# Gate and up products as three rounded products, value projections among the first maxima of attention, fewer and larger transfers of keys and rows of maxima

## The chip, the cores and the metric

The kernel runs on one core of a Trainium2 chip. Its time is the device time of one execution in microseconds, the median of several runs; lower is better. One further execution is profiled, and its trace is what the rows below come from.

## The reference, cut to what matters

A residual stream `x` of 2048 tokens by 256 features passes eight layers. What the change touches:

```python
# first layer (A): attention, 16 heads of 16; masked scores become zero and stay in the softmax
scores = einsum('bthd,bshd->bhts', q, k) * tril
out = einsum('bhts,bshd->bthd', softmax(scores / T ** 0.5), v).reshape(B, T, 256) @ Wo
# feed-forward, run twice (after A, and after the linear layer)
gate = einsum('bsd,hd->bsh', x, w_gate)          # hidden 1024
up = einsum('bsd,hd->bsh', x, w_up)
y = einsum('bsh,dh->bsd', silu(gate) * up, w_down)
# linear layer ("lin"): k * v summed over the tokens so far, times q, then a projection
# differential attention (B): every token sees every other; two score products with a factor lambda
# attention with latent keys and rotary parts (C): causal
# hyperbolic layers ("hyp", "hypout"): one projection, scaled by a tanh of its norm
```

Every layer is added to `x`, and its input is `x` normalised per token. All is float32.

## The kernel before

**Stages.** The program is written out in order: `start` (normalisation "in" and the projections "p0" of A), attention A, a wave of "o0", "ffn", "lin", "ffn", then the projections "p1" of B, attention B, a wave of "o1", "hyp", "p2", attention C, and "o2" with "hypout". Outside attention the tokens go in four chunks of 512 (`NC` = 4, `CH` = 512). In a wave, each layer follows the one before by two chunks, so that TensorE has another layer's chunk while a normalisation runs on VectorE. A chunk's normalised input is transposed on TensorE (`norm_transposes`, after the main work of the next step) and copied by ScalarE to `HT` (`norm_copies`).

**Feed-forward.** For each of eight blocks `m` of 128 hidden features, TensorE makes a gate bank and an up bank of PSUM, each from two float32 products of 128x512 (`over_k`, line 740). A float32 product stands in the trace as two records. ScalarE takes a tanh of the gate (L1035), VectorE makes the gated product in two instructions (L1196, L1200), and line 842 multiplies by the down weights. Four banks go round.

**Projections p0, p1.** TensorE makes four banks of queries and keys (`PARTS_ORDER`) and two of values (`token_major` into `VV`, four float32 products of 128x256 in each bank). VectorE splits every bank of queries and keys into a rounded part and a rest (L1169, L1170) in one of two buffers `STG`, and SyncE's queue (SP) stores both in DRAM; VectorE may fill a buffer only when its store has landed. From there SP loads queries (`load_q`, 6 transfers for a cell) and keys (`load_k`, 12 transfers of 64 KB for each half of the heads and each chunk). A matmul on tiles of type float32r reads numbers already rounded, and makes one record.

**Attention.** A cell is a chunk of 512 queries and a group of four heads; 16 cells follow each other. `Layer.plan` writes one list, `steps`, which all engines walk: "max" (TensorE makes two banks of scores, line 885, and VectorE takes their maxima, L1289 or L1292; two slots of two banks), "neg" (GpSimd negates and splits the 16 maxima of a token, `NM`), "mtr" (TensorE transposes them, line 895, ScalarE copies them to `MR`), after which SP writes them as two more rows of the queries (`max_rows`, 4 transfers a cell, line 502), "score" (line 924: scores minus their maximum, then exp by ScalarE, L1054), "pv" (line 953: times the values), and "otr", "rec", "suf" at the end of a cell. TensorE keeps the order of the list: the first "score" of a cell waits for that cell's rows of maxima, and what stands behind it waits too. The rows of ones that go with the keys are written by `one_rows`, once for each half.

**SP before the first score of a layer** goes through: keys of the last chunk (first half), ones of the second half, a wait for everything ScalarE has taken, queries of the fourth slot (into a part of `HT`), keys of the second half (one chunk of them for A and C, all four for B), then the rows of maxima of cell 0. Weights for the hyperbolic layers are loaded right after attention A, 15 transfers (lines 563 to 571).

Of the kernel before, what the change touches and what calls it, by code (L numbers as in the profile page):

```python
# [23 lines left out]
F32 = mybir.dt.float32  # L24
# [7 lines left out]
P = 128  # L32
# [7 lines left out]
HG = 4  # L40
# [40 lines left out]
class Layer:  # L81
# [59 lines left out]
    def plan(self):  # L141
# [46 lines left out]
        self.steps += due[0][at:]  # L188
        self.ring, self.at, self.n_taken = {}, {}, 0
# [8 lines left out]
def build(nc, a, out):  # L198
# [3 lines left out]
    with ctx:  # L202
# [29 lines left out]
        NEG = sb("NEG", [P, HG, BPC])  # L232
        OT4 = OS[:, 0:BPC * HG * VW].rearrange("p (b j d) -> p b j d", b=BPC, j=HG)
# [5 lines left out]
        NM = sb("NM", [P, HG, PARTS, BPC])  # L239
# [11 lines left out]


# [86 lines left out]
        mask_low = sem("mask_low")  # L339
# [14 lines left out]
        HAS_NORM = {"in", "o0", "ffn", "lin", "o1", "hyp", "o2"}  # L354

# [7 lines left out]
        BANKS = {"in": (0, 0), "wt": (0, N_TRANSPOSED), "p0": (4, 2), "p1": (4, 2), "p2": (8, 3), "o0": (2, 2), "o1": (2, 2), "o2": (2, 2),  # L363
                 "ffn": (18, 0), "lin": (6, 2), "hyp": (2, 0), "hypout": (2, 0)}
        D_COUNT, A_COUNT, HT_AT = {}, {}, []
        NORM_OF = {}
        d_total, a_total = 0, 0
        for kind, steps in PROGRAM:
            if steps is None:
                D_COUNT[kind], A_COUNT[kind] = d_total, a_total  # L370
                continue
# [20 lines left out]
        K_DMAS = 16 * 12  # L392
        Q_DMAS = 16 * 6
        ROW_DMAS = 16 * HG
# [12 lines left out]
        def _(sp):  # L407
# [86 lines left out]
            def max_rows(L, n):  # L494
# [3 lines left out]
                k = PARTS * BPC  # L498
# [19 lines left out]

            def attention(L):
# [34 lines left out]
            for kind, steps in PROGRAM:  # L554
                if steps is None:
                    attention(att[kind])
                    if kind == "A":

                        sp.wait_ge(L0.out_done, len(L0.cells))
                        for dst, src in ((W2["q"], km(a["L1b_q"])), (W2["o"], km(a["L1b_o"])), (WN, km(a["hyp_w"])),  # L560
                                         (SCALE, a["hyp_scale"].partition_broadcast(P)),
                                         (WKV, km(a["kv"])), (WKUP, a["kup"]), (WVUP, a["vup"])):
                            sp.dma_start(dst, src).then_inc(w2_in, 16)
                        half = ROPE // 2
                        for i in range(2):
                            for h in range(2):
                                o = half * (h if i == 0 else 1 - h)
                                dst = slice(o, o + half)
                                src = slice(half * h, half * (h + 1))
                                sp.dma_start(WQR[i][:, :, dst], km(a["qr"])[:, :, src]).then_inc(w2_in, 16)  # L570
# [812 lines left out]
```

## Time and profile before

| | us |
|---|---|
| median of 3 runs | 2762.98 |
| lowest and highest of them | 2744.1, 2763.98 |
| profiled execution, its time | 2726.22 |
| its span, first to last instruction | 2724.5 |
| TensorE busy | 2514.2 (92%) |
| VectorE busy | 1836.6 (67%) |
| ScalarE busy | 1332.6 (49%) |
| GpSimd busy | 239.1 (9%) |
| mean granted TensorE clock | 0.931 |

The profiled execution took 36.8 us less than the median. Sums made on the trace stand against 2726.22 us; what they give is then taken off the median.

### The profile page before, as it was taken

Reading aid. Unit: us, or ns where it says so; the run is one execution under the profiler, and the core shown is the slowest. Engines: PE = TensorE matmul, PEld = TensorE weight load, DVE = VectorE, ACT = ScalarE, POOL = GpSimd, SP = SyncE. Lnnn points to the kernel's source line nnn. Section 1 sums busy time; section 2 is a strip of 40 time slices with the busy share of each in tenths; the row PEclk is TensorE's granted clock in tenths of the full one; section 3 lists DMA queues with packets and bytes.
Section 4 is the critical chain, followed back from the end, with each engine's and each line's share of the span. In section 5 each row is a group of like instructions: output and inputs, shape, how many; then the busy total and the mean of one; then the engine's idle time right before and its main releaser. Section 6 shows DMA issues by size and latency. Waiting matters only on the chain.

```text
span 2724.5 us, 46506 instructions
## 1 busy us (share of the span) xinstructions
PE 2514.2 (92%) x17992; PEld 1253.4 (46%) x17992; DVE 1836.6 (67%) x4042; ACT 1332.6 (49%) x2678; POOL 239.1 (9%) x767
## 2 busy tenths in 40 slices
PE   7699999989999998899999999976879999999995
PEld 5354444445655564244444444343345544444444
DVE  5557788815355535899999999658657676666508
ACT  2246677861111110388888888840035444455551
POOL 0332212110000000000000000000022111010100
PEclk9568799999999998599999999997789999999998
DMA  8410000000000006300000000002721000000000
GB/s 248 107 32 18 13 13 8 2 20 1 1 0 1 16 0 187 55 13 7 14 13 8 13 8 7 2 16 77 214 66 31 13 15 8 7 2 7 5 29 32
DMA packets 61407, 90.55 MB, mean 33 GB/s; under 512 B 13441, under 2 KB 25985, under 8 KB 61057
## 3 DMA queue, kind: packets, MB, share of 16 engines
q1 hardware_dynamic: 61184, 87.57, 11.6%
q8 instruction: 142, 2.33, 0.3%
q14 instruction: 81, 0.66, 0.1%
HBM read 54.76 MB, written 31.46 MB: 32 GB/s over the span
## 4 chain that ended last, share of the span: by engine, by line
PE 74%; DVE 13%; SPq 4%; ACT 3%; DMA 3%; issue 2%; POOL 0%; DVEq 0%; POOLq 0%; ACTq 0%
PE PS L953 19%; PE PS L885 14%; PE PS L740 13%; PE PS L924 11%; PE PS L935 7%; PE PS L842 4%; DVE MP L1292 3%; ACT PF L1054 3%; PE PS L933 2%; SPq L476 2%; DVE WC L1289 1%; DVE JUNK L1289 1%; DVE ST L1126 1%; SPq L487 1%; DVE KF L1133 1%
## 5 line engine op out<-in xcount | busy, mean ns | idle before, releaser
L1054 ACT ACTIVATE PF<-PS 128x512 f32<-128x512 f32 (+3 forms) x2304 | 1169.3, 560 | 618.2 <-PE PS L935 341.1
L1292 DVE TENSOR_REDUCE MP<-PS 128x2 f32<-128x1024 f32 x704 | 849.5, 1222 | 80.2 <-PE PS L885 74.6
L953 PE MATMUL PS<-PF,VX 128*32 128x256 f32 (+3 forms) x9216 | 708.4, 385 | 0.1
L885 PE MATMUL PS<-KFR,QRR 48*128 48x512 f32 (+3 forms) x1920 | 487.5, 512 | 55.5 <-DVE MP L1289 17.1
L924 PE MATMUL PS<-QRR,KFR 50*128 50x512 f32 (+3 forms) x1920 | 405.3, 418 | 30.6 <-DMA QRR<-MR 14.0
L885 PEld LDWEIGHTS PS<-KFR,QRR 48*128 48x128 f32 x1920 | 191.2, 199 | 406.7 <-issue 240.9
L953 PEld LDWEIGHTS PS<-PF,VX 128*32 128x32 f32 x9216 | 190.5, 110 | 337.0 <-issue 238.4
L924 PEld LDWEIGHTS PS<-QRR,KFR 50*128 50x128 f32 x1920 | 187.8, 192 | 113.3 <-ACT PF L1054 90.1
L740 PE MATMUL PS<-HT,WA 128*128 128x512 f32 x512 | 221.1, 592 | 0.0
L935 PE MATMUL PS<-WAR 128*128 128x512 f32 (+3 forms) x640 | 215.5, 418 | 0.0
L1289 DVE CUSTOM_DVE_ANT_0 JUNK<-PS,WB 128x512 bf16<-128x512 f32 (+2 forms) x224 | 131.3, 586 | 114.9 <-PE PS L885 99.5
L670 POOL TENSOR_SCALAR_AFFINE_SELECT PF<-PF 128x128 f32<-128x128 f32 x512 | 142.5, 292 | 549.0 <-ACT PF L1054 544.4
L740 PEld LDWEIGHTS PS<-HT,WA 128*128 128x128 f32 x512 | 96.6, 190 | 118.6 <-issue 115.7
L935 PEld LDWEIGHTS PS<-WAR 128*128 128x128 f32 x640 | 95.8, 189 | 97.3 <-issue 90.7
L997 ACT COPY HT<-PS 128x512 f32<-128x512 f32 x64 | 34.6, 588 | 213.9 <-PE PS L774 213.9
L1289 DVE CUSTOM_DVE_ANT_0 WC<-PS,WB 128x512 bf16<-128x512 f32 (+2 forms) x224 | 130.1, 581 | 0.0
L1141 DVE TENSOR_TENSOR X<-PS,X 128x512 f32<-128x512 f32 x48 | 33.1, 690 | 135.4 <-PE PS L842 99.5
L1035 ACT ACTIVATE PF<-PS 128x512 f32<-128x512 f32 x64 | 38.2, 597 | 167.5 <-PE PS L740 167.5
L933 PE MATMUL PS<-WAR 64*128 64x512 f32 (+3 forms) x320 | 116.7, 365 | 0.0
L933 PE MATMUL PS<-WCR,WAR 64*128 64x512 f32 (+3 forms) x320 | 116.6, 364 | 0.0
L842 PE MATMUL PS<-WA,KF 128*128 128x256 f32 x512 | 111.8, 379 | 0.0
L1289 DVE CUSTOM_DVE_ANT_0 JUNK<-PS,X 128x512 bf16<-128x512 f32 (+1 forms) x96 | 64.2, 669 | 63.3 <-PE PS L885 60.1
(139 smaller groups left out, 2223.2 us busy)
## 6 DMA issues: line engine op xcount, KB each, us to landing
KFR<-parts_a_k SPq DMA_DIRECT2D x96, 64.0 KB, 3.1
KFR<-parts_b_k SPq DMA_DIRECT2D x96, 64.0 KB, 3.6
KFR<-parts_c_k SPq DMA_DIRECT2D x96, 64.0 KB, 3.1
QRR<-parts_a_q SPq DMA_DIRECT2D x78, 64.0 KB, 2.3
QRR<-parts_b_q SPq DMA_DIRECT2D x78, 64.0 KB, 2.3
QRR<-parts_c_q SPq DMA_DIRECT2D x78, 64.0 KB, 2.3
parts_a_q<-PF SPq DMA_DIRECT2D x8, 512.0 KB, 3.8
parts_a_k<-PF SPq DMA_DIRECT2D x8, 512.0 KB, 3.7
```

Of the source, the lines that this page charges most:

```text
L476: sp.dma_start(x.rearrange("d (r t) -> d r t", r=PAIRS)[:, :, t], head_rows(L, "k", PRODUCTS[product][1], h, g, t))\
L670: g_.affine_select(out=tile, in_=tile, compare_op=ALU.is_ge, fill=0.0, base=0, pattern=[[1, P]], channel_multiplier=-1).then_inc(L.mask_do ...
L740: ins = mm(dst, left(k), right(k), start=k == 0, stop=k == n - 1)
L842: ins = mm(bank(b, D, i * D), GT[:, m, blk(2 * h + i)], WDT[:, m, :], start=m == 0, stop=m == HID // P - 1)
L885: ins = mm(bank(slot + h, w), Q[rows, t0:t0 + P], KS[rows, o:o + w], start=True, stop=True)
L924: ins = mm(bank(4 + (e + h) % RING2, CH - off), KS[rows, o:o + P], Q[rows, t0 + off:t0 + CH], start=True, stop=not L.rope)
L933: mm(bank(4 + (e + h) % RING2, CH - off), RS[half, ROPE_K[1], sb_ * P:(sb_ + 1) * P], q, start=False, stop=False)
L935: mm(bank(4 + (e + h) % RING2, CH - off), RS[:, ROPE_K[0], sb_ * P:(sb_ + 1) * P], RS[:, ROPE_Q[0], c * CH + off:(c + 1) * CH], start=Fals ...
L953: ins = mm(PS[32 * j:32 * j + 2 * DH, 7 * CH + t0:7 * CH + t0 + size], VX[:, v0:v0 + 2 * DH], PT[:, u % SETS, j, t0:t0 + size], start=firs ...
L1054: sc.activation(PT[:, u % SETS, j, off:CH], bank(4 + e % RING2, CH - off), ACT.Exp).then_inc(L.taken, 1)
L1289: ins = v.tensor_tensor_reduce(out=junk[h][:, 0:w], in0=src[:, h], in1=other, scale=1.0, scalar=low, op0=ALU.mult if L.zeros else ALU.add, ...
L1292: ins = v.reduce_max(dst, src, AX.X)
```

## The change

**Gate and up.** Each float32 product becomes three float32r products of the same 128x512 shape: rounded weights with rounded input, rounded weights with the input's rest, the weights' rest with rounded input. The rounded weights `WGU[0]` are made by ScalarE, one 128x512 copy in each of the first eight units of A's last cell. The rests `WGU[1]` are made by GpSimd, eight 128x512 subtractions after its last step of A. For the chunks that feed a feed-forward layer (normalisations after "o0" and "lin"), `norm_copies` takes each transposed bank twice, once rounded and once whole (into unused room in the values' tile), and GpSimd subtracts (two 128x512 for a chunk). TensorE waits for `wgu_ready` once and for `ht_rest` before each feed-forward chunk.

**Values.** p0 and p1 no longer make the values. They are eight steps ("value", c, h) spread over the steps before the first "mtr" of A and B: one bank each, four float32 products of 128x256, and a copy by ScalarE. SP loads the fourth slot of queries only after they are all taken, and so does TensorE start its first "mtr".

**Transfers.** `load_k` issues 6 transfers of 128 KB for a half and a chunk instead of 12 of 64 KB; `max_rows` issues 2 instead of 4 (`NM` is laid out by halves for it).

**Order on SP.** Keys of the second half now come before the fourth slot of queries. For B the ones of the first half are written again, since the rounded weights lay there, and the 15 transfers of hyperbolic weights move from the end of A to between B's fourth slot of queries and B's first rows of maxima.

```diff
+        if not self.rope:
+            products = [("value", c, h) for c in range(NC) for h in range(BPC // 2)]
+            room = self.steps.index(("mtr", 0)) - 1
+            for i, step in reversed(list(enumerate(products))):
+                self.steps.insert(1 + i * room // len(products), step)
...
+        WGU = [KS[:, i * 4096:(i + 1) * 4096] for i in range(2)]
+        HTL = [QS[:, i * KD * CH:(i + 1) * KD * CH].rearrange("p (k t) -> p k t", k=KD) for i in range(3)]
+        HTL.append(WCR[:, 0:KD * CH].rearrange("p (k t) -> p k t", k=KD))
...
-                    for g in (2 * half, 2 * half + 1):
-                        x = KS[row:row + DH, g * PAIRS * T:(g + 1) * PAIRS * T].bitcast(F32)
-                        sp.dma_start(x.rearrange("d (r t) -> d r t", r=PAIRS)[:, :, t], head_rows(L, "k", PRODUCTS[product][1], h, g, t))\
-                            .then_inc(L.k_in[half][c], 16)
+                    x = KS[row:row + DH, half * 2 * PAIRS * T:(half + 1) * 2 * PAIRS * T].bitcast(F32).rearrange("d (x t) -> d x t", t=T)
+                    src = scr[L.name, "k"][PRODUCTS[product][1], half * 2 * HG * DH:(half + 1) * 2 * HG * DH, t]
+                    sp.dma_start(x[:, :, t], src.rearrange("(x h d) t -> h d x t", h=2, d=DH)[h]).then_inc(L.k_in[half][c], 16)
...
-                for j in range(HG):
-                    row = HALF * (j % 2) + MROW
-                    dst = Q_AT[L.q_slot[n][0]][row:row + PARTS, j // 2 * CH:(j // 2 + 1) * CH].bitcast(F32)
-                    sp.dma_start(dst.rearrange("i (n t) -> i n t", t=P), MR[j * k:(j + 1) * k, :]).then_inc(L.max_rows_in, 16)
+                for h in range(2):
+                    row = HALF * h + MROW
+                    dst = Q_AT[L.q_slot[n][0]][row:row + PARTS].bitcast(F32)
+                    sp.dma_start(dst.rearrange("i (x t) -> i x t", t=P), MR[h * k:(h + 1) * k, :]).then_inc(L.max_rows_in, 16)
...
                 one_rows(1, ones_in[1 + "abc".index(L.name)])
-                sp.wait_ge(a_free, A_COUNT[L_KEY[L.name]])
-                load_q(L, QRING - 1)
+                if L is L1:
+                    one_rows(0, ones_back)
+                sp.wait_ge(a_free, A_BEFORE[L_KEY[L.name]])
                 load_k(L, 1, 0)
                 if not L.causal:
                     for c in range(1, NC):
                         load_k(L, 1, c)
+                sp.wait_ge(a_free, A_COUNT[L_KEY[L.name]])
+                load_q(L, QRING - 1)
+                if L is L1:
+                    hyperbolic_weights()
...
+                        for i in range(8):
+                            w = slice(i * CH, (i + 1) * CH)
+                            pool.wait_ge(wgu_high, i + 1)
+                            g_.tensor_tensor(WGU[1][:, w], WA[:, w], WGU[0][:, w].bitcast(F32), ALU.subtract).then_inc(wgu_ready, 1)
...
+                        for kk in range(KD):
+                            by_head = lambda x: x.rearrange("p (b h d) -> p b h d", h=H, d=DH)
+                            g_.tensor_tensor(by_head(low[:, kk, :]), whole(pending[1], pending[0], kk),
+                                             by_head(HTR[:, pending[0], kk, :].bitcast(F32)), ALU.subtract).then_inc(ht_rest, 1)
...
                     for m in range(HID // P):
-                        for W in (WGT, WUT):
+                        for w in range(2):
                             b = d_bank()
-                            over_k(bank(b), lambda kk: W[:, kk, m * P:(m + 1) * P], ht).then_inc(d_ready, 1)
+                            for kk in range(KD):
+                                o = w * 2048 + kk * HID + m * P
+                                high, rest = WGU[0][:, o:o + P], WGU[1][:, o:o + P]
+                                mm(bank(b), high, HTR[:, c, kk, :], start=kk == 0, stop=False)
+                                mm(bank(b), high, low[:, kk, :], start=False, stop=False)
+                                ins = mm(bank(b), rest, HTR[:, c, kk, :], start=False, stop=kk == KD - 1)
+                            ins.then_inc(d_ready, 1)
...
+                    if step[0] == "value":
+                        _, c, h = step
+                        W, b = (W0 if L is L0 else W1A)["v"], a_bank()
+                        for i in range(2):
+                            t0 = (2 * h + i) * P
+                            ins = over_k(bank(b, D, i * D), lambda kk: HT[:, c, kk, t0:t0 + P], lambda kk: W[:, kk, :])
+                        ins.then_inc(a_ready, 1)
...
+                    if kind in SPLIT:
+                        take(HTR[:, c, k, :], bank)
+                        na.k -= 1
+                        take(whole(kind, c, k), lambda b: bank(b).rearrange("p (b h d) -> p b h d", h=H, d=DH)).then_inc(a_free, 1)
...
+                        if L.zeros and n == len(L.cells) - 1 and r == 1 and u - L.first[n] < 8:
+                            w = slice((u - L.first[n]) * CH, (u - L.first[n] + 1) * CH)
+                            sc.copy(WGU[0][:, w], WA[:, w]).then_inc(wgu_high, 1)
```

## Rows read from the trace of the kernel before

**Rows 1.** Stretches by stage: length, busy of each engine, granted clock, DMA share, GB/s

```profile
75.00:103.00 28.00, 10.38 (x35) 4.84 (x35) 15.44 (x71) 0.60 (x3) 11.97 (x18) 0.51 0.61 133
617.00:1025.00 408.00, 402.57 (x1315) 239.29 (x1314) 192.30 (x493) 57.85 (x100) 1.94 (x8) 1.00 0.01 3
...
1079.00:1124.00 45.00, 30.52 (x79) 11.33 (x81) 43.68 (x40) 0.25 (x1) 0.67 (x3) 0.50 0.73 127
```

**Rows 2.** Chain of waits, first feed-forward chunk, gate and up: start, length, line, records

```profile
617.62 27.47 PE PS L740 x64
```

**Rows 3.** Timeline of TensorE in C: four rounded products in a row, and two

```profile
2139.13 1.19 PE L745 MATMUL PS<-WAR 128*128 128x512 f32 x4
...
2421.45 0.73 PE L935 MATMUL PS<-WAR 128*128 128x512 f32 x2
2422.11 0.64 PE L953 MATMUL PS<-PF,VX 128*32 128x256 f32 x8
```

**Rows 4.** Timeline of p1: VectorE's wait for a store, SP's load of queries

```profile
1041.20 8.24 SPq L487 DMA_DIRECT2D QRR<-parts_b_q  x18
...
1052.79 0.69 DVE L1169 TENSOR_SCALAR PF<-PS 128x512 fp32r<-128x512 f32 x1 [9.94 <-DMA parts_b_q<-PF]
```

**Rows 5.** Timeline of A's start: transposed maxima, SP's queue, first score

```profile
86.68 5.90 SPq L487 DMA_DIRECT2D HTR<-parts_a_q  x6
...
87.86 0.25 ACT L1063 COPY MR<-PS 32x128 f32<-32x128 f32 x1 [11.12 <-PE PS L895]
...
98.31 2.57 SPq L502 DMA_DIRECT2D QRR<-MR  x4
...
102.03 0.80 PE L924 MATMUL PS<-QRR,KFR 50*128 50x512 f32 x2 [10.70 <-DMA QRR<-MR]
```

**Rows 6.** Timeline of p1 and of B's start: values, maxima, SP's queue, first score

```profile
1043.47 3.62 PE L740 MATMUL PS<-WB,HT 128*128 128x256 f32 x16
...
1096.00 22.86 SPq L476 DMA_DIRECT2D KFR<-parts_b_k  x48
...
1107.37 9.13 DVE L1292 TENSOR_REDUCE MP<-PS 128x2 f32<-128x1024 f32 x8
...
1118.99 2.62 SPq L502 DMA_DIRECT2D QRR<-MR  x4
...
1123.62 0.79 PE L924 MATMUL PS<-QRR,KFR 50*128 50x512 f32 x2 [1.42 <-DMA QRR<-MR]
```

**Rows 7.** Timeline after A: first and last of 15 transfers; copies of the first input

```profile
595.68 0.39 SPq L563 DMA_DIRECT2D WC<-in_L1b_q  x1
...
604.11 0.49 SPq L571 DMA_DIRECT2D WC<-in_kr  x1
...
610.24 1.07 ACT L997 COPY HT<-PS 128x512 f32<-128x512 f32 x2 [5.65 <-PE PS L774]
```

**Rows 8.** Timeline of C's start: transposed maxima, keys on SP, the wait

```profile
1965.46 5.44 SPq L476 DMA_DIRECT2D KFR<-parts_c_k  x12
...
1975.54 0.25 ACT L1063 COPY MR<-PS 32x128 f32<-32x128 f32 x1 [15.66 <-PE PS L895]
...
1983.55 5.55 SPq L476 DMA_DIRECT2D KFR<-parts_c_k  x12
...
1991.61 0.48 PE L885 MATMUL PS<-KFR,QRR 48*128 48x128 f32 x2 [12.01 <-DMA KFR<-parts_c_k]
```

**Rows 9.** Groups of instructions: busy, mean ns, idle before; a copy, a GpSimd addition

```profile
L997 ACT COPY VX<-PS 128x512 f32<-128x512 f32 x24 | 14.1, 586 | 152.9 <-PE PS L740 152.9
L635 POOL TENSOR_TENSOR WC<-WC,VX 128x272 f32<-128x272 f32 x24 | 18.2, 760 | 1.6
```

**Rows 10.** Stretches of attention A, columns as in the first group

```profile
560.00:572.00 12.00, 10.96 (x108) 3.43 (x100) 0.00 (x0) 10.27 (x20) 0.20 (x1) 1.00 0.01 1
...
133.00:188.00 55.00, 53.43 (x340) 30.89 (x344) 29.44 (x77) 22.30 (x57) 16.60 (x48) 0.50 0.14 37
215.00:256.00 41.00, 38.45 (x390) 18.77 (x390) 34.58 (x81) 27.01 (x63) 12.21 (x41) 1.00 0.07 21
```

More of the change, by code:

```diff
@@ L238, in build @@
         MX = sb("MX", [P, 2, HG, BPC])
[L239 removed]
+        NM = sb("NM", [P, 2, PARTS, PAIRS, BPC])
         EM = sb("EM", [P, 2, HG, BPC])
@@ L250, in build, with whole @@
         bank = lambda b, n=CH, o=0: PS[:, b * CH + o:b * CH + o + n]
+        WGU = [KS[:, i * 4096:(i + 1) * 4096] for i in range(2)]
+        HTL = [QS[:, i * KD * CH:(i + 1) * KD * CH].rearrange("p (k t) -> p k t", k=KD) for i in range(3)]
+        HTL.append(WCR[:, 0:KD * CH].rearrange("p (k t) -> p k t", k=KD))
+        def whole(kind, c, k):
+            b = 2 * (KD * (SPLIT[kind] + c % 2) + k)
+            return VV[:, b:b + 2, :, 0:DH]
         GT = QF[:, 0:4096].rearrange("p (m t) -> p m t", t=CH)
@@ L369, in build @@
             if steps is None:
-                D_COUNT[kind], A_COUNT[kind] = d_total, a_total
+                D_COUNT[kind], A_BEFORE[kind] = d_total, a_total
+                if not att[kind].rope:
+                    a_total += NC * BPC // 2
+                A_COUNT[kind] = a_total
                 continue
@@ L517, in load_rope_q, with hyperbolic_weights @@
                 sp.dma_start(RQ2[ROPE:P, c % 2, :].bitcast(F32), scr_r["q"][0][:, t]).then_inc(L.rope_q_in[c % 2], 16)
+            def hyperbolic_weights():
+                sp.wait_ge(L0.out_done, len(L0.cells))
+                for dst, src in ((W2["q"], km(a["L1b_q"])), (W2["o"], km(a["L1b_o"])), (WN, km(a["hyp_w"])),
+                                 (SCALE, a["hyp_scale"].partition_broadcast(P)),
+                                 (WKV, km(a["kv"])), (WKUP, a["kup"]), (WVUP, a["vup"])):
+                    sp.dma_start(dst, src).then_inc(w2_in, 16)
+                half = ROPE // 2
+                for i in range(2):
+                    for h in range(2):
+                        o = half * (h if i == 0 else 1 - h)
+                        dst = slice(o, o + half)
+                        src = slice(half * h, half * (h + 1))
+                        sp.dma_start(WQR[i][:, :, dst], km(a["qr"])[:, :, src]).then_inc(w2_in, 16)
+                        sp.dma_start(WKR[i][:, dst], a["kr"][:, src]).then_inc(w2_in, 16)
             def attention(L):
@@ L556, in _ @@
                     attention(att[kind])
[L557 to L570, printed above, removed]
-                                sp.dma_start(WKR[i][:, dst], a["kr"][:, src]).then_inc(w2_in, 16)
                     continue
@@ L979, in _ @@
                     if pending is not None:
-                        norm_of[c] = pending
+                        norm_of[c] = pending, k
+                    if k in SPLIT:
+                        rest_of[c] = rests.next()
                 assert pending is None
@@ L998, in take, with take_values @@
                 return sc.mul(dst, src, scale)
+            def take_values(c, h):
+                b0 = BPC * c + 2 * h
+                take(VV[:, b0:b0 + 2, :, 0:DH], lambda b: bank(b).rearrange("p (b h d) -> p b h d", h=H, d=DH)).then_inc(a_free, 1)
             def weight_copies():
@@ L1023, in main @@
                     take(CKV[:, c % 2, :], lambda b: bank(b)[0:LATENT]).then_inc(a_free, 1)
-                if k in ("p0", "p1", "p2"):
+                if k == "p2":
                     for h in range(2):
-                        b0 = BPC * c + 2 * h
-                        take(VV[:, b0:b0 + 2, :, 0:DH], lambda b: bank(b).rearrange("p (b h d) -> p b h d", h=H, d=DH)).then_inc(a_free, 1)
+                        take_values(c, h)
                 if k == "ffn":
@@ L1038, in main, with norm_copies @@
                     sc.activation(NW[:, 5, :], NW[:, 4, :], ACT.Tanh).then_inc(n2_tanh, 1)
-            def norm_copies(c):
+            def norm_copies(c, kind):
                 for k in range(KD):
-                    take(HT[:, c, k, :], bank).then_inc(a_free, 1)
+                    if kind in SPLIT:
+                        take(HTR[:, c, k, :], bank)
+                        na.k -= 1
+                        take(whole(kind, c, k), lambda b: bank(b).rearrange("p (b h d) -> p b h d", h=H, d=DH)).then_inc(a_free, 1)
+                    else:
+                        take(HT[:, c, k, :], bank).then_inc(a_free, 1)
             def attention(L):
@@ L1057, in attention @@
                             sc.activation(EM[:, n % 2], MX[:, n % 2], ACT.Exp, scale=-1.0).then_inc(L.weight_done, 1)
+                    if step[0] == "value":
+                        take_values(*step[1:])
                     if step[0] == "mtr":
@@ L1088, in _ @@
                     if pending is not None:
-                        norm_copies(pending)
-                    pending = c if k in HAS_NORM else None
+                        norm_copies(*pending)
+                    pending = (c, k) if k in HAS_NORM else None
         @block.vector
```

44 lines of the change are left out of this document (29 added, 15 removed).

## The prediction

> **What bounds the kernel now.** I read the stretches by stage first [rows 1]. In the first feed-forward wave TensorE is busy 402.6 of 408 us at full granted clock: what it saves there is saved. At the starts of attention A and B it is busy 10.4 of 28 and 30.5 of 45 us at half clock: something else sets the pace. The chain of waits shows gate and up of a feed-forward chunk as one unbroken piece [rows 2]. The timelines then say what ends last elsewhere. In p1 VectorE waits 9.94 us for a store that SP could issue only behind 18 loads of queries [rows 4]. In A the transposed maxima lie in `MR` at 88.1, but SP still issues queries and then keys and comes to them at 98.31; TensorE idles 10.70 us and scores at 102.03 [rows 5]. In B VectorE's maxima set the pace, and SP is through its 48 loads of keys at 1118.9, just in time for the rows of maxima at 1118.99 [rows 6]. In C the maxima are ready at 1975.8, and TensorE waits for keys to 1991.6 [rows 8].
>
> **Gate and up.** Now 64 records take 27.47 us, 0.429 each: two passes of 512 columns [rows 2]. After, it is 96 records a chunk of one pass each. Price of one: four rounded 128x512 products on 128 rows last 1.19 us together and two last 0.73, so each further one costs (1.19 - 0.73)/2 = 0.23 us [rows 3]. 96 x 0.23 = 22.1 us, 5.4 less; eight chunks (four in each of two runs) give **-43 us**. The lower end, half a float32 record (0.215), gives 20.6 us and -55; the upper end is rival 1. I take 0.23, the row of the same shape.
> The Trainium skill ("TensorE: Matmul & The Clock Gate", Back-to-back issue gap) gives column count over 2.4 GHz plus about 2.5 ns, 216 ns; by it the term would be -54. The trace's four in a row disagree with it by 14 ns each, and the trace decides.
> VectorE and ScalarE don't become the bound: they are busy 192 and 58 of the wave's 408 us [rows 1]. Down and the normalisations stay.
>
> **Making the halves.** In A's last cell ScalarE makes 20 exps, five units of four, in 12 us, and is busy 10.27: 2.05 of each unit of 2.4 [rows 10]. Eight units get a copy of 0.586 more [rows 9]. Between nothing left over (all fits the idle 0.35 but 0.24, so 2) and 8 x 0.586 = 4.7, I take **+4**: the exps feed three banks in a ring, so the idle time is in slivers. Nothing at all is its lowest end.
> GpSimd's eight subtractions: 272 columns take 0.760 [rows 9], so 512 some 1.43, together 11.5 us from A's end near 596 [rows 7], to 608. The first chunk's transposed input is copied by 611.3 now [rows 7], by 612.5 with two copies more; two subtractions end near 615.5, before TensorE's first gate product at 617.6 [rows 2]: hidden by 2 us. The same two copies delay the "o0" chunk behind them once. Together **+1.5**, ends 0 and 5. Later chunks have a whole step of cover, 14 us or more. If that cover were gone at the first chunk, it would cost what rival 4 says.
> No row shows GpSimd beside a VectorE instruction with two SBUF inputs. The Trainium skill ("SBUF — State Buffer", SBUF: two separate sides) says that such a pair takes turns for a whole instruction; the short steps of the normalisation before 617 are of this kind. By it two to four turns of 1.43 would be added, 3 to 6 us once.
>
> **Values.** Removed from p0 and p1: 3.62 us of TensorE a chunk, some 1.7 a bank [rows 6]. It lies beside VectorE's wait for stores [rows 4], so taking it away gives nothing there. Added: eight banks before the first "mtr".
> *A.* Eight values and nine maxima. TensorE has idled before, so the clock starts at half (0.51 in this stretch [rows 1]). Two values at half clock are 6.8, six at full 10.3, the maxima and what lies between some 3.5: from 74.4 the last value is copied at about 95.5. Before, TensorE sat idle until 102, so most of this is free. SP has waited: queries 2.9, two rows 1.3, landing 1.1 (102.03 less the end of SP's 2.57, 100.88 [rows 5]), first score near 101 against 102.03: **-1**. Ends: all values at full clock, 96 (-6); all at half, 112 (+10).
> *B.* Here VectorE paces: a maximum each 1.14 us (9.13/8 [rows 6]). TensorE works one maximum ahead, which covers about 1.2 us of a value; a value costs VectorE 1.7 - 1.2 = 0.5 at full clock and 3.4 - 1.2 = 2.2 at half. At the mean, 1.35 x 8 = 10.8 us. Thirty maxima stand before or between the values: 1079.4 + 34 + 10.8 = 1124 for the last one. Behind its copy (0.6) SP issues, in order: six transfers of queries (22.86/48 = 0.48 each, 2.9), the 15 of hyperbolic weights (595.68 to 604.60, 8.9 [rows 7]), two rows of maxima 1.3, and the landing 2 (1123.62 less 1121.61 [rows 6]). That is 1124 + 15.7 - 1 (p1, below) = 1139, against 1123.6: **+15**, ends +8 and +22. Behind the waiting score stand all further maxima, so VectorE stops too; nothing makes this up.
>
> **Transfers.** A transfer of 64 KB costs SP 0.48 us, one of 4 KB 0.64 (2.57/4 [rows 5]): its size doesn't show, so I take 0.48 for 128 KB; the bound is 0.96, no saving. In p0 and p1 most waits end with a landing of the same bytes: -1 each, in the two sums above. In C, between 1965.46 and the rows of maxima, 24 loads of keys become 12 and 4 rows 2: 12 x 0.47 + 2 x 0.64 = 6.9, all on the path, since the maxima are ready at 1975.8 [rows 8]. Within p2 SP's queue is in the way now and then: -2. C: **-9**, ends 0 and -12. Other late rows of maxima, half as many transfers each: **-2**.
>
> **Sum.** -43 + 4 + 1.5 - 1 + 15 - 9 - 2 = -34.5 us; the profiled execution would be 2726.2 - 34.5 = 2692, the median 2763 - 34 = **2729 us**. About 1% (27 us) is what a measurement of this kernel can tell from no change: its runs lie 20 us apart, the profiled one 37 below the median. One likely reason stands in the trace: A has long stretches at either clock, and does 390 matmuls in 41 us at full, 340 in 55 at half [rows 10]. By that 55 us at half are worth about 19.
>
> **Rivals.**
> 1. *The weights don't hide (slower than before).* The stage breaks even when a rounded product costs 27.47/96 = 0.286 us, the whole sum at 0.274. Two rounded products take 0.66 from their start to the next matmul, 0.33 each [rows 3]; if all 96 paid that, a chunk would take 31.7 us, +4.2 x 8 = +34 in place of -43, and the median would be 2806. Against it: the further ones of a row cost 0.23 in the same rows, so the 0.33 holds one exposed weight load and not two.
> 2. *The waits of B and A eat the gain.* Half clock throughout the first maxima: A +10, B +22, the rest as above: -16 us, 2747. For it: both stretches stand near 0.50 now, though TensorE was busy two thirds of B's. Against: the values are dense work.
> 3. *The starts cost little, a rounded product 0.22.* A -6, B +8, gate and up -50: -53 us, 2710. Earlier full clock in A would add to it.
> 4. *GpSimd is late.* At twice its row, 31 us for ten subtractions in place of 14.4, +14 at the wave's start: 2743.
>
> **How the numbers follow.** Forecast as summed 0.48; rival 3 and beyond (clocks in A, down to 2680) 0.20; rivals 2 and 4 together 0.24; rival 1 0.08. Of the forecast's own spread (2713 to 2745) two thirds lie below 2735, the 1% line, and of rivals 2 and 4 a sixth: faster 0.32 + 0.20 + 0.04 = 0.56. Slower by over 1% (above 2790): rival 1 and a hundredth of bad clocks, 0.09. The same: 0.35. The range leaves out rival 1 and the far ends: 2682 to 2765.
>
> **What the profile after would show.** Chain of waits: gate and up near 22.1 us a chunk, 96 records; 31.7 would be rival 1. From the first maximum to the first score some 26 us in A, as now, and 60 us in B in place of 44, with the hyperbolic transfers right before the rows of maxima on SP. C's keys of the second half some 7 us sooner. A first gate product at most 5 us later behind A's end; a wait on GpSimd there would be rival 4. What would make me wrong: another price of a rounded product in a dense stream, a clock that doesn't rise under the values, a 128 KB transfer that costs SP twice as much, or long stretches of A at another clock than now.

## The result and the profile after

The changed kernel takes 2788.64 us (median of 12 runs) against 2763.22 us for the kernel before on the same chip (12 runs): 1.0116 times as long, interval 1.0082 to 1.0149. It is slower by 1.2%, where 2729 us was forecast. Every ratio compares fast executions alone, those within 1.5% of a kernel's fastest (one of 5169 us, whose cause isn't known, is left out here), and the profiled executions of e1 and e2 were slower ones with mean clocks of 0.907 and 0.900, so that of these two no attention's time is used.

The profiled execution took 2766.02 us (span 2764.3), 39.8 us above that of before. To see where, I took the start of the first instruction of each stage from the timelines of both kernels:

| stage | before | after | change | forecast |
|---|---|---|---|---|
| start to A's first score | 102.03 | 103.05 | +1.0 | -1 |
| A, first score to end | 493.85 | 495.67 | +1.8 | +4 |
| A's end to first gate product | 21.6 | 25.2 | +3.6 | +1.5 |
| first gate product to end of last down | 407.2 | 391.95 | -15.3 | -43 |
| last down to B's first maximum | 54.7 | 78.8 | +24.2 | -1 |
| B's first maximum to first score | 44.2 | 68.1 | +23.9 | +16 |
| B, first score to end | 672.9 | 666.5 | -6.4 | (-2, all rows of maxima) |
| B's end to C's first score | 196.5 | 199.1 | +2.6 | -9 |
| C and what is behind it | 731.5 | 735.8 | +4.4 | 0 |

The two stages before B's first score cost 48.1 us together, three times what the feed-forward wave gives back. Outside the three attentions the profiled executions of all kernels agree within some 4 us in a stage where nothing was edited, so this table tells more than the whole time does; the +2.6 before C's first score is within that spread by itself.

The stretches by stage, as [rows 1] of before (us, busy of TensorE, weight loads, VectorE, ScalarE, GpSimd, granted clock, DMA share, GB/s):

```profile
624.00:1016.00 392.00, 368.57 (x1565) 288.36 (x1564) 205.12 (x492) 64.22 (x114) 18.25 (x22) 0.99 0.01 3
1016.00:1095.00 79.00, 33.25 (x81) 14.20 (x79) 28.62 (x57) 2.15 (x4) 0.00 (x0) 0.74 0.68 176
1095.00:1163.00 68.00, 47.13 (x143) 26.48 (x145) 44.19 (x39) 4.97 (x9) 0.67 (x3) 0.68 0.36 58
```

In the wave TensorE now has 23 us without work, where it had 5 [rows 1]. Its groups of instructions there (busy, mean ns, idle before and what ended it) name the place, and VectorE's groups name a second thing:

```profile
L879 PE MATMUL PS<-HTR,KFR 128*128 128x512 f32 x256 | 104.7, 409 | 13.3 <-DVE PF L1268 13.3
```
```profile
L1186 DVE TENSOR_SCALAR NW<-NW 128x4 int32<-128x4 int32 x13 | 8.8, 678 | 0.4
L1200 DVE TENSOR_SCALAR NW<-MV 128x4 f32<-128x4 f32 x13 | 8.7, 668 | 0.4
```

The timeline of one such stall, on GpSimd, VectorE and TensorE:

```profile
625.94 2.37 POOL L742 TENSOR_TENSOR QRR<-VX,HTR 128x512 fp32r<-128x512 f32 x2 [6.31 <-ACT VX L1055]
```
```profile
626.27 0.90 DVE L1200 TENSOR_SCALAR NW<-MV 128x4 f32<-128x4 f32 x1
627.20 1.13 DVE L1186 TENSOR_SCALAR NW<-NW 128x4 int32<-128x4 int32 x1
628.36 0.17 DVE L1187 TENSOR_SCALAR NW<-NW 128x4 int32<-128x4 int32 x1
...
630.34 1.38 DVE L1205 TENSOR_SCALAR KF<-X,MV,NW 128x256 f32<-128x256 f32 x4
631.64 0.68 DVE L1268 SCALAR_TENSOR_TENSOR PF<-PF,PS 128x512 f32<-128x512 f32 x1
```
```profile
632.37 0.50 PE L879 MATMUL PS<-HTR,KFR 128*128 128x512 f32 x1 [2.59 <-DVE PF L1268]
```

TensorE is one step ahead: it fills the four banks of gate and up while VectorE still normalises another chunk, and then waits until VectorE comes to the first of them (L1268). While GpSimd's two subtractions run, two VectorE instructions on four columns take 0.90 and 1.13 us; the third, behind them, takes 0.17. Only 7 of the 13 normalisations in the wave meet a subtraction; the others take what they took before.

The stalls cost more than their own length. There are six of 2.5 to 2.8 us in the wave, and at the end of three of them (from 719.9, 818.9 and 849.6 us) the granted clock falls to the lower of its two levels, 1.2 GHz, for a few us. The first of these, right behind a wait of 2.55 us for L1268 (columns as above):

```profile
720.00:724.00 4.00, 4.00 (x12) 3.09 (x12) 1.94 (x4) 0.60 (x1) 0.00 (x0) 0.58 0.01 4
```

Gate products start 0.43 us apart there and 0.235 before and behind. The three stretches last 10.2 us together and so cost about 5 us, an estimate from these two rates. In the kernel before and in e5 below the clock stays at 2.4 GHz through the wave.

At B's start the timeline of SP and of TensorE (as [rows 6]) and the chain of waits between them say what ends last:

```profile
1070.88 5.92 SPq L496 DMA_DIRECT2D KFR<-parts_b_k  x8
1076.84 8.26 SPq L456 DMA_DIRECT2D KFR<-ONE  x4
1085.15 13.38 SPq L496 DMA_DIRECT2D KFR<-parts_b_k  x24
1148.61 2.63 SPq L506 DMA_DIRECT2D HTR<-parts_b_q  x6
...
1160.09 1.41 SPq L521 DMA_DIRECT2D QRR<-MR  x2
```
```profile
1094.75 0.79 PE L932 MATMUL PS<-KFR,QRR 48*128 48x512 f32 x2 [33.89 <-DMA KFR<-ONE]
1095.47 3.62 PE L778 MATMUL PS<-WB,HT 128*128 128x256 f32 x8
...
1138.57 1.99 PE L778 MATMUL PS<-WB,HT 128*128 128x256 f32 x8
...
1162.83 0.80 PE L980 MATMUL PS<-QRR,KFR 50*128 50x512 f32 x2 [5.68 <-DMA QRR<-MR]
```
```profile
1078.22 4.29 SPq L456
1082.55 11.85 DMA KFR<-ONE
1094.75 0.79 PE PS L932 x2
```

B's first maximum waits for the ones that are written again; they are issued behind all keys of the first half, and the last lands 11.85 us after its issue. Then come the values: seven of eight banks take 2.9 to 3.8 us, one 1.99. In the gap between 1151.25 and 1160.09 stand the 15 hyperbolic weights. C's start, as [rows 8]:

```profile
2007.76 6.95 SPq L496 DMA_DIRECT2D KFR<-parts_c_k  x6
...
2017.65 1.30 SPq L521 DMA_DIRECT2D QRR<-MR  x2
```
```profile
2026.49 0.47 PE L932 MATMUL PS<-KFR,QRR 48*128 48x128 f32 x2 [13.99 <-DMA KFR<-parts_c_k]
2028.44 0.80 PE L980 MATMUL PS<-QRR,KFR 50*128 50x512 f32 x2 [1.47 <-DMA QRR<-MR]
```

SP's six transfers of second-half keys took 6.95 us in place of 5.55 for twelve, and TensorE still waits for keys long after SP has issued them. The first score then waits for the rows of maxima, which SP has issued by 2018.9.

### The profile page after: what moved, and what is told of

Same layout as the page of the kernel before. It is cut to its first block, busy times and chain, and to the rows that moved or that the text cites. A ratio compares the mean times of both kernels' runs of the same rounds, so it can differ in the third digit from the quotient of the medians.

```text
span 2764.3 us, 46832 instructions
## 1 busy us (share of the span) xinstructions
PE 2481.3 (90%) x18248; PEld 1306.1 (47%) x18248; DVE 1852.4 (67%) x4042; ACT 1345.0 (49%) x2702; POOL 268.5 (10%) x791
## 4 chain that ended last, share of the span: by engine, by line
PE 70%; DVE 16%; DMA 4%; ACT 4%; issue 3%; SPq 2%; POOL 1%; DVEq 0%; POOLq 0%; ACTq 0%
PE PS L1009 19%; PE PS L932 14%; PE PS L980 10%; PE PS L991 7%; PE PS L778 5%; PE PS L889 4%; DVE MP L1364 3%; ACT PF L1121 3%; PE PS L989 2%; PE PS L879 2%; PE PS L880 2%; PE PS L881 2%; DVE ST L1198 1%; DVE KF L1205 1%; DVE WC L1361 1%
## 5 line engine op out<-in xcount | busy, mean ns | idle before, releaser
L932 PE MATMUL PS<-KFR,QRR 48*128 48x512 f32 (+3 forms) x1920 | 475.4, 501 | 88.0 <-DMA KFR<-ONE 33.9
L778 PE MATMUL PS<-HT,WB 128*128 128x512 f32 x224 | 105.6, 623 | 20.4 <-DVE PF L1242 20.1
L1055 ACT COPY VX<-PS 128x512 f32<-128x512 f32 x40 | 23.8, 595 | 205.5 <-PE PS L778 205.5
L879 PE MATMUL PS<-HTR,KFR 128*128 128x512 f32 x256 | 104.7, 409 | 13.3 <-DVE PF L1268 13.3
L702 POOL TENSOR_SCALAR NEG<-MX 128x16 f32<-128x16 f32 x48 | 12.2, 254 | 1009.7 <-DVE MX L1374 916.4
```

What stands on the lines that cost most here:

```text
L778: ins = mm(dst, left(k), right(k), start=k == 0, stop=k == n - 1)
L879: mm(bank(b), high, HTR[:, c, kk, :], start=kk == 0, stop=False)
L932: ins = mm(bank(slot + h, w), Q[rows, t0:t0 + P], KS[rows, o:o + w], start=True, stop=True)
```

## The experiments

Theory 1 was: the loss is the ones' wait (+22 to 24), the values at half clock (some +15) and the weights on SP (+9) at B's start; gate and up give less because VectorE lets four banks fill, GpSimd making it worse; the merged transfers give nothing since landing, not issue, sets C's start. Ratios are to the kernel before; stage times are those of the table above. Kernels that ran once (e5 to e8) have no ratio.

**e1_ones_in_p1**

```diff
                 one_rows(1, ones_in[1 + "abc".index(L.name)])
-                if L is L1:
-                    one_rows(0, ones_back)
...
                         project(k, c, d0)
+                    if (k, c) == ("p1", 0):
+                        one_rows(0, ones_back)
```

> The kernel after with one edit: the two transfers that write the rows of ones of the first half of the keys again are issued in p1 behind the stores of chunk 0 instead of behind the last keys. Theory 1 (their landing, 11.85 us in the chain behind 4.3 us of issue, holds back B's first maximum): the 33.89 us idle before B's first product falls to about 12, first maximum some 22 us sooner, and the ratio to the kernel before falls from 1.012 to about 1.004. Rival (the maxima would meet the values at half clock and SP's queue of queries and weights anyway, so the chain behind only waits longer): first score at most 8 us sooner, ratio 1.009 or more.

Ratio 1.0048 (1.0013 to 1.0083). Last down to first maximum 57.2 us (after: 78.8). The first maximum's row:

```profile
1093.12 0.80 PE L932 MATMUL PS<-KFR,QRR 48*128 48x512 f32 x2 [9.62 <-DVE PF L1242]
```

It now waits for VectorE and no DMA. The stage behind it took 70.2 us (68.1 in after), so of 21.6 us all but 2 came through. Theory 1 holds, the rival falls. From last down to first maximum it is still 2.5 us longer than before the change (54.7).

**e2_values_in_p.** The eight "value" steps are taken out of A and B, and `token_major(...)` for the values and its two copies stand in p0 and p1 again, as in the kernel before.

> The kernel after with the value products back in p0 and p1, all else as after. Theory 1 (a value among the first maxima costs VectorE up to 2 to 3 us each at half clock, and nothing in p1): first maximum to first score in B falls from 68 us to about 52, the first maximum stays within 2 us, A within 2 us; ratio about 1.006. Rival (the transfers end last there anyway): B's first score within 4 us of before this edit, ratio 1.010 or more. Second rival (p1 becomes longer by the values): the first maximum 4 to 14 us later, nothing gained.

Ratio 1.0026 (0.9988 to 1.0064). B's first maximum to first score 43.0 us, 25.1 less than after; last down to first maximum 79.6, so the values cost less than 1 us in p1. More came back than the 16 expected: without values the 15 weights are issued while VectorE works through the maxima, and they cost nothing either:

```profile
1118.41 0.42 SPq L545 DMA_DIRECT2D WC<-in_L1b_q  x1
...
1135.75 0.48 SPq L553 DMA_DIRECT2D WC<-in_kr  x1
1151.37 1.41 SPq L522 DMA_DIRECT2D QRR<-MR  x2
```

**e7_values_kept** tells the two apart. Edit: e1's, and

```diff
                 load_q(L, QRING - 1)
-                if L is L1:
-                    hyperbolic_weights()
                 for n in range(len(L.cells)):
                     max_rows(L, n)
+                    if L is L1 and n == 0:
+                        hyperbolic_weights()
```

> The kernel after with two edits: ones of the first half in p1, and the hyperbolic weights behind the first rows of maxima; the values stay among the first maxima. Of the 68 to 70 us from B's first maximum to its first score, theory 1 gives 9 to the 15 transfers of weights on SP and some 16 to values at half clock: 60 us remain. Rival (the values alone set it, the weights are issued under them or under the landing of queries): 66 us or more remain.

61.0 us remained: as theory 1 said. So 7 us (68.1 - 61.0) are the weights, or 9 (70.2 - 61.0) against e1, which differs from e7 in them alone; they stand on the path only because the values hold SP up before them. The other 17.5 (61.0 less e4's 43.5) are the values.

**e3_merged_alone.** The kernel before with the change's `load_k`, `max_rows` and layout of `NM` alone.

> The kernel before with nothing but the merged transfers (six loads of 128 KB for twelve of 64 KB of keys, two transfers for four of rows of maxima, with the order of the rows of NM that these need). Theory of the prediction (SP's issue sets the path, 0.48 us a transfer): C's keys of the second half some 7 us sooner, ratio 0.996. Theory 1 (the landing of the bytes sets it: a 128 KB transfer lands in about 5.0 us, a 64 KB one in 3.1): last store to first score of C within 2 us of before, ratio 0.999 to 1.001.

Ratio 1.0034 (0.9998 to 1.0071), no gain; B's end to C's first score 198.9 us against 196.5, which alone is within the spread of such stages. The last piece of it tells more. In every kernel with merged transfers but e8, whose order differs, C's first maximum and first score lie 30.8 to 31.6 us apart, in the seven with single ones and the old order (before, e4, e5, e6, e9, e10, e11) 28.3 to 29.0. The DMA view of the last 30 us before C's first score (packets; then packets, MB and the time they took as a share of 16 engines), before and e3:

```profile
DMA packets 2767, 4.09 MB, mean 136 GB/s; under 512 B 684, under 2 KB 972, under 8 KB 2766
...
q1 hardware_dynamic: 2766, 4.09, 61.6%
```
```profile
DMA packets 2766, 4.35 MB, mean 140 GB/s; under 512 B 532, under 2 KB 820, under 8 KB 2764
...
q1 hardware_dynamic: 2764, 4.34, 87.9%
```

As many packets and about as many bytes, at about the same GB/s, but they took 88% of the engines' time instead of 62%. In the last 30 us before C's first score that share is 90 to 94% in every kernel with merged transfers and 54 to 65% in every one without. It isn't pure work (in after it reads 1.05 from 2013 to 2026), so it can hold time in which a packet stands behind others; why each takes longer is open. What it did to the path stands in the chains of waits, before and e3:

```profile
1991.23 1.73 DMA QRR<-MR
1993.01 0.80 PE PS L924 x2
```
```profile
1994.89 10.33 DMA QRR<-MR
2005.27 0.79 PE PS L967
```

From C's first maximum to the end of the rows' issue SP needed 27.2 us before and 21.2 in e3: the issue did shrink, by 6 us. The landing of the rows grew from 1.73 to 10.33 us. The Trainium skill ("DMA: Bandwidth & Descriptors", Rules for kernel authors) advises joining many small transfers into one; from 64 to 128 KB no run here shows a gain from it.

**e4_split_alone.** The kernel before with gate and up from halves alone: e1's and e7's edits, values in p0 and p1 (e2), `load_k` and `max_rows` as before.

> The kernel before with gate and up from rounded halves alone: values in p0 and p1, all transfers as before, the ones of the first half issued in p1 behind chunk 0's stores, and the hyperbolic weights in B behind the first rows of maxima, off the first score's path. Theory of the prediction: 8 x 5.4 us of gate and up less 5.5 of making the halves, -37 us, ratio 0.986. Theory 1 (0.24 us a product, and TensorE, now faster, waits with four full banks for VectorE's normalisation of another chunk in every second chunk; the wave starts 3.7 us later): chunks of 23.2 and 26 us in turn, -20 us and +4, ratio 0.994.

Ratio 0.9982 (0.9938 to 1.0026). A's end to first gate 25.2 us, first gate to last down 391.97: both the same as in after to 0.02 us, so all that the change saves and loses there is the split's. Theory 1's -20 was some 5 too much for the wave. The prediction's 0.986 is outside the interval; theory 1's 0.994 is just inside, and no change at all is inside too.

**e5_gpsimd_moved.** e4, and in GpSimd's program:

```diff
                         pool.wait_ge(a_free, HT_AT[NORM_OF[pending[1], pending[0]]])
+                        if pending != (0, "o0"):
+                            pool.wait_ge(norm_ready, NORM_OF[pending[1], pending[0]] + 2)
...
+                        i = u - L.first[n]
+                        if L.zeros and n == len(L.cells) - 1 and r == 1 and i < 8:
+                            w = slice(i * CH, (i + 1) * CH)
+                            pool.wait_ge(wgu_high, i + 1)
+                            g_.tensor_tensor(WGU[1][:, w], WA[:, w], WGU[0][:, w].bitcast(F32), ALU.subtract).then_inc(wgu_ready, 1)
```

> The split alone, with GpSimd's work moved: it makes the second halves of an input only after VectorE's next normalisation is done (but for the first), and those of the weights unit by unit within A's last cell. Theory 1 (GpSimd's subtractions hold up VectorE's tensor_scalar instructions of four columns, 1.1 us each instead of 0.17, two for each normalisation, and so lengthen the stall with four full banks; eight subtractions behind A's end delay the wave's start): these instructions take 0.17 us, a stalled chunk of gate and up falls from 26.6 us by 1 to 2, A's end to first gate product from 25.2 to 22 or less, first gate to last down from 391.95 to some 385. Rival (the stall is VectorE's own chain of steps and the copies by ScalarE set the wave's start): chunks within 0.3 us, start within 1 us.

VectorE's two instructions are at 0.17 us again:

```profile
L1193 DVE TENSOR_SCALAR NW<-NW 128x4 int32<-128x4 int32 x13 | 2.2, 171 | 0.4
L1207 DVE TENSOR_SCALAR NW<-MV 128x4 f32<-128x4 f32 x13 | 2.2, 170 | 0.4
```

From first to last product the eight chunks take 25.2, 23.5, 26.7, 23.2, 26.7, 23.3, 25.4, 23.2 us in after, and 23.2 to 23.5 each here. The longest wait of TensorE in a chunk falls from as much as 2.8 us to 0.6 to 0.9. The chunks give 11.0 us together, the pieces between them (the linear layer above all) 5.6, and the wave takes 375.4 us (391.95 with the clash): 16.6 us less where theory 1 had 7. About 5 of the 16.6 are the clock's, which no longer falls within the wave; theory 1 had no such term. The wave's start took 23.0 us against 25.2, but that isn't the edit. These stretches hold the start in after, in e9 (this same kernel) and in e12, which has both edits too (columns as above):

```profile
599.00:624.00 25.00, 19.48 (x89) 15.81 (x88) 15.49 (x54) 5.47 (x11) 12.35 (x11) 0.83 0.00 1
```
```profile
596.00:619.00 23.00, 17.32 (x87) 14.24 (x88) 15.37 (x54) 5.24 (x11) 2.87 (x3) 0.93 0.00 1
```
```profile
600.00:625.00 25.00, 19.48 (x88) 15.73 (x88) 15.45 (x54) 5.43 (x11) 2.56 (x3) 0.83 0.00 1
```

25 us go with a clock of 0.83 and 23 with 0.93, wherever GpSimd makes the weights' halves (its 12.35 us of work are 2.56 in e12). Two more kernels say the same: e7, with GpSimd's work behind A's end as in after but a clock of 0.93, took 23.5 us, and e3, without any split, 23.5 at 0.82. For the start the rival holds, for the chunks theory 1.

**e6_short_norm.** e5 with `for _ in range(1)` for the three Newton steps of `rsqrt`: two of the three are left out.

> The kernel e5_gpsimd_moved with one Newton step in place of three in each inverse square root (two steps are left out, so the output is less exact). Each normalisation is six small VectorE instructions of about 0.2 us shorter. Theory 1 (TensorE, at 0.235 us a product, fills its four banks in 5.6 us while VectorE normalises another chunk; what exceeds that is lost): the stalls of gate and up end nearly, chunks 22.5 to 23.5 us, 1.2 us less on each that still stalled. Rival (the long chunks come from the halved clock or from the products themselves): chunks as in e5_gpsimd_moved within 0.3 us.

Every chunk takes 22.3 to 22.4 us and no product waits for VectorE; the wave takes 368.0. 22.35/95 is 0.235 us a product. So the price of a product in the dense stream was near the forecast's 0.23, and what exceeded it was the wait for VectorE and the clock behind it. Theory 1 holds.

**e8_rows_first.** after, with `one_rows(1, ...)` and `load_k(L, 1, 0)` of A and C behind `max_rows(L, 0)`.

> The kernel after with one edit: in A and C SP issues the first rows of maxima before the ones and keys of the second half (which are first used two cells later). Theory 1 (in C the DMA engines are the limit, 99% busy in the window with 128 KB transfers landing 5.6 us after their issue; rows of maxima ready at 2008.7 wait behind 0.9 MB of keys): the first score of C comes 10 us or more sooner after the last store, A's up to 5 us sooner. Rival (the keys of the first half, which the first maxima need, land last anyway): C's first score at most 3 us sooner, VectorE's maxima wait for them.

C's first maximum to first score 29.2 us in place of 31.6, A's 27.0 as before: the rival. TensorE does the third cell's first maxima before the first score, and they need the second half's keys, whatever SP issues first:

```profile
2039.03 0.48 PE L935 MATMUL PS<-KFR,QRR 48*128 48x128 f32 x2 [13.43 <-DMA KFR<-parts_c_k]
```

**e9_gpsimd_moved_timed**

> The kernel e5_gpsimd_moved again, now timed. From its profile: A's end to last down 398.4 us against 428.8 before, p1 3 us longer, the rest as before: -27 to -30 us, ratio 0.990. Rival (what the stages save is lost to a lower granted clock in the attentions, which stood at 0.917 against 0.931 in the profiled executions): ratio 0.996 or more.

Ratio 0.9965 (0.9937 to 0.9993). Outside the three attentions the profile shows 876.8 us against 900.9 before, -24.1, near what was expected. The ratio shows -10 us, its interval -2 to -17: less than the forecast, and the rival's number. The granted clock in the attentions accounts for most of the gap: between first score and end, C took 656.8 us at a clock of 0.994 in the profile of before, 669.2 at 0.969 here, with the same instructions; A took 492.9 us in e9 at a clock of 0.859 and 529.2 in e4 at 0.777. The timed executions agree. Over those of e9 and before that enter the ratio, time falls by some 18 us for each 0.01 of mean granted clock; the clocks were 0.914 for e9 and 0.921 for before on average, and at an equal clock e9's lie some 28 us below. That is an estimate, since an edit that takes away work at full clock moves the mean clock by itself. Whether the edit lowers the clock in the attentions, or the executions drew it so, is not shown.

**e10_queries_spread.** e5, with `load_q(L, n)` issued at chunk 1's stores n = 0, 1, 2 instead of three together ahead of the first.

> The kernel e5_gpsimd_moved with the 18 loads of queries in p0 and p1 issued six behind each of the first three stores of chunk 1, instead of all ahead of the first. Theory 1 (in p1 VectorE and TensorE wait for the store behind 8 to 10 us of issue of loads): last down to first maximum of B falls from 57 us to 50, p0 by some 3; ratio 0.3 percentage points below e9. Rival (the stores and key loads behind them, all on one queue, take the same time in any order): within 2 us.

Ratio 1.0009 (0.9976 to 1.0042); last down to first maximum 57.7 us, unchanged: the rival. The code is shared with p2, which the expectation left out, and there it costs: B's end to C's first maximum 175.1 us instead of 167.7. By what wait is open.

**e11_ones_by_scalar.** e10 with the two `KS<-ONE` transfers issued by ScalarE at ("p1", 1).

> The kernel e10 with the two transfers of ones issued by ScalarE's queue in p1, chunk 1, instead of by SP. In the split alone SP's issue of the loads right behind the ones took 0.72 and 2.01 us in place of 0.42. Theory 1 (the slow issue is SP's own queue taking up the many small pieces of the ones): p1 2 to 3 us shorter, no SP issue above 1 us. Rival (the DMA engines are held up whoever issues): slow landings stay, p1 within 1 us.

Ratio 0.9966 (0.9929 to 1.0004); p1 57.6 us: the rival. SP's next loads are slow although ScalarE issued the ones (timelines of ScalarE and of SP):

```profile
1028.70 1.92 ACTq L1085 DMA_DIRECT2D KFR<-ONE  x2
```
```profile
1032.55 5.15 SPq L507 DMA_DIRECT2D QRR<-parts_b_q  x6
```

The next two groups of six take 3.20 and 3.23 us, and before the change 18 loads took 8.24 there, 2.75 for six. So it isn't SP's own queue taking up the ones; what it is stays open.

**e12_rows_first_too.** e11 with e8's edit.

> The kernel e11 with the edit of e8 as well: first rows of maxima ahead of the ones and keys of the second half in A and C. With 64 KB transfers and the values in p0, theory 1 (in A rows of maxima then wait for nothing but the landing; in C the first maxima of the third cell stand before the first score and wait for the second half's keys whatever the order): A's first maximum to first score from 25.4 us to 18, C's within 3 us, ratio 0.3 points below e11. Rival (A's third cell asks for the second half's keys just as early as C's): A within 2 us, nothing gained.

Ratio 0.9941 (0.9905 to 0.9976): faster than before by 0.6%. It is the lowest ratio here, but the intervals of e9 and e12 overlap, and the profile favours e9: outside the attentions it takes 876.8 us and e12 880.8. At an equal clock, by the same estimate as for e9, e12 gains 17 us and e9 28. A's first maximum to first score 16.4 us instead of 25.5, C's 31.1 instead of 28.3. In A the maxima lie in `MR` at 91.4, and the score comes at 95.3:

```profile
91.49 2.60 SPq L522 DMA_DIRECT2D QRR<-MR  x4
94.13 1.29 SPq L457 DMA_DIRECT2D KFR<-ONE  x2
```

So the values in A had hidden a gain that this order gives: e8 has them, ends its last value product at 96 and gained nothing there. e5 with A's rows first and nothing else of e10 to e12 should be better still, by the 7.4 us of p2 and the 2.8 of C; that is an estimate, and no run shows it.

## Why the prediction was wrong

**Making the halves and the wave's start.** The copies in A's last cell: its first eight units took 24.25 us instead of 21.52, +2.7 for the +4. GpSimd's eight subtractions took 9.84 us in all, less than the 11.5 estimated, and were hidden, as the moved ones of e12 show. At a clock of 0.93 (before had 0.92 in that stretch) the start takes 23.0 to 23.5 us, +1.4 to +2.0 where +1.5 was forecast; the rest of after's +3.6, about 2 us, goes with the lower clock, since e3 without a split takes 23.5 at 0.82. The prediction's sentence on VectorE and GpSimd taking turns looked in too narrow a place: at the start alone, and at instructions with two SBUF inputs. The rows show it for `tensor_scalar` with one, and all through the wave: the 13 normalisations behind the first gate product took 13 us more on VectorE ((678 + 668 - 2 x 170) ns x 13), some 1.9 us for each of the 7 that met a subtraction. The Trainium skill ("SBUF — State Buffer", Who interferes with whom) names `tensor_scalar` among the operations that can take the shared port pair; by that, and by 0.90 and 1.13 us in the rows, the trace agrees.

**Gate and up: the step that failed is "VectorE and ScalarE don't become the bound: they are busy 192 and 58 of the wave's 408 us".** An average over the wave says nothing on four banks in a stretch of 7 us. At 0.43 us a record four banks last 6.9 us (16 x 0.429). A normalisation with the residual ahead of it and the first gate operation behind it takes VectorE 6.9 us in e5 (623.05 to 629.99 in its timeline), so before the change the two just met. Now four banks last 5.6 us (24 x 0.235), and with GpSimd's clash VectorE needs 8.6 (623.69 to 632.32 in the stall shown). So -43 became -15.3 for the wave: without the clash it is -31.8 (e5, 407.2 to 375.4), and with a shorter normalisation besides -39.2 (e6, 368.0). The prediction also took the full clock for granted; the three drops behind the stalls are some 5 us of what the clash cost. What was forecast for the products alone, 22.1 us a chunk, is what e6 has (22.35).

**p1 and B's start: the step was missing.** The part on values gives p1 "-1", and no term prices the new `pe.wait_ge(ones_back, ...)` or says what SP issues ahead of it. It was worth 21.6 us of the stage (e1, 78.8 to 57.2), the largest loss from one line of the change, and next to gate and up's missing 27.7 the largest miss of the sum. It was in the diff and could be read: the last thing issued, with TensorE's first product of B behind it.

**Values in B: mis-sized.** VectorE waited 0.7 to 3.1 us at each of the eight values, 18.5 in all in its timeline, in place of 1.35 each: seven of the eight ran wholly or mostly at the lower clock. The values cost 17.5 us for the 10.8, the weights 7 to 9 for the 8.9. Rival 2's upper end (+22) is near what this stage gave (+23.9), but its sum kept the -43 and had no wait for the ones. A's start was as forecast but for 2 us: there the clock did rise under the values, to 0.87 in the stretch from 75 to 103 us. (Rival 4's ten subtractions at twice their row are 28.6 us, not 31; its +14 goes with 28.6.)

**Transfers in C: the landing was taken as constant.** The term was right that SP's issue set the path before, and the issue did shrink (27.2 to 21.2 us from C's first maximum, e3). But it left the landing at what it was. With merged transfers the rows of maxima landed 10.33 us after their issue in place of 1.73, and that took back the 6 us and 2.6 more: +2.6 in place of -9. The price of an issue was wrong too: a 128 KB transfer cost SP 0.56 us at B's start (13.38 for 24) and 1.16 in C (6.95 for six), above the 0.96 that the prediction named as no saving.

**The attentions.** The forecast's "other late rows of maxima -2" and the rest can't be told from the clock's changes: A's stage ran from 493 to 529 us over kernels whose attention steps are the same (e9 and e4).

## What to carry to other kernels

When an engine is made faster, don't ask how busy its neighbours are over the stage; ask how long its buffers last at the new pace against the neighbour's longest single piece of work. For every wait that a diff adds, find the producer's place in its queue and what stands ahead of it, and price that first. Move GpSimd's SBUF work to where VectorE is idle or reading PSUM, and when transfers are joined, ask whether the landing still is what it was once they are issued sooner.

## What the runs showed of the hardware

- A GpSimd subtraction of 512 columns in SBUF (1.17 to 1.27 us) holds up VectorE's `tensor_scalar` of four columns until it is done: 0.17 us becomes 0.90 to 1.14. Instructions with one input in PSUM, beside the same subtractions, took their usual 0.68 to 0.69 (605.18 in after; L1275 and L1279, eight times each, in e5), and a scan with two SBUF inputs (L1290 in e5) 1.77 in place of 1.26, twice.
- A dense stream of rounded 128x512 products goes at 0.235 us each at full clock (e6); four in a row in C showed 0.23 [rows 3].
- Behind the two transfers that write rows of ones, SP issues the next loads more slowly, whichever engine issued the ones: one took 2.0 us in e4, and six took 5.15 in e11 in place of 2.75. The cause is open.
- With 128 KB transfers in place of 64 KB ones and as many packets, the packets took 88% of the DMA engines' time in place of 62%, for 4.35 MB in 31 us against 4.09 in 30, and a load of keys landed after 6.1 us (median) in place of 2.9 (e3).
- At the end of three of the six waits of 2.5 to 2.8 us in after's wave, in an otherwise dense stream, the granted clock fell from 2.4 to 1.2 GHz for a few us; in e5, where TensorE's longest wait is 1.8 us, it never did.
- A granted clock of 0.83 in place of 0.93 at the wave's start is worth 2 us of 23; 0.969 in place of 0.994 over C is worth 12 of 657. It changes between executions of one kernel: C took 674.9 us at 0.959 in e5 and 669.2 at 0.969 in e9.
